# A fused layer on one core: two tiles' statistics first, pair 0's keys in other PSUM banks, and another order of the transfers ahead of the expert loop

## The reference

```
g = x[:, :, curve[:, 1], curve[:, 0]]                 # 256 pixels of each image
h = concat([einsum('bcn,ec->bne', g, proj_w) + proj_b, txt], 1)   # 4 x 768 x 192
n = layernorm(h)
Q, K, V = xpos(n @ Wq), xpos(n @ Wk), n @ Wv          # 6 heads, 128 / 64
s = Q K^T / sqrt(128) * decay_mask                    # causal, no softmax
a = groupnorm(s V) * silu(n @ Wg) @ Wo
h = h + a
n = layernorm(h)
z = n P[s]                                            # 8 sub-layers of rank 16
w = softmax(top4(z C[s]^T))                           # 4 of 64 experts
y = sum_k w_k (gelu(z W1[k] + b1) W2[k] + b2)
out = h + gelu(concat_s y @ G1 + g1b) @ G2 + g2b
```

## Time and profile before

| | us |
|---|---|
| median of 3 runs | 892.36 |
| lowest, highest | 890.64, 892.42 |
| the profiled execution | 895.4 |
| its span | 893.6 |

### The profile page before, as it was taken

The page is one execution under the profiler, slowest core; times in us unless marked ns, Lnnn a source line. Parts: engine busy times, 40 slices in busy tenths (PEclk is TensorE's granted clock), DMA queues, the critical chain, the costliest instruction groups (busy, mean ns, idle before and its releaser), DMA issues.

```text
span 893.6 us, 16290 instructions
## 1 busy us (share of the span) xinstructions
PE 847.4 (95%) x5430; PEld 393.1 (44%) x5430; DVE 661.7 (74%) x1609; ACT 593.3 (66%) x901; POOL 528.8 (59%) x481
## 2 busy tenths in 40 slices
PE   8799999999999986998999999999999999999997
PEld 3477777777778755222223222322232223222222
DVE  5666666565476776888878887888788887877774
ACT  2243333335542472989897989798979897988784
POOL 0456565445365633575957595759575767575552
PEclk9999999999999998799999999999999999999998
DMA  9600002000000078889878887988788888889772
GB/s 257 235 1 1 2 2 76 2 1 1 1 2 16 15 113 197 252 251 264 247 225 258 270 252 234 262 269 246 248 249 273 251 270 249 267 268 285 246 253 98
DMA packets 90116, 154.28 MB, mean 173 GB/s; under 512 B 30329, under 2 KB 56377, under 8 KB 89644
## 3 DMA queue, kind: packets, MB, share of 16 engines
q1 hardware_dynamic: 90034, 153.25, 58.3%
HBM read 138.96 MB, written 15.83 MB: 173 GB/s over the span
## 4 chain that ended last, share of the span: by engine, by line
PE 75%; ACT 11%; DVE 7%; DMA 3%; issue 3%; SPq 1%; POOL 0%; DVEq 0%; POOLq 0%; ACTq 0%
PE ps L917 17%; PE ps L854 17%; PE ps L512 5%; PE ps L893 5%; PE ps L535 3%; PE ps L520 3%; PE ps L608 3%; PE ps L545 2%; PE ps L599 2%; ACT ring L1253 2%; DMA wbc<-w_rows 2%; PE ps L577 2%; PE ps L687 1%; PE ps L656 1%; PE ps L708 1%
## 5 line engine op out<-in xcount | busy, mean ns | idle before, releaser
L1958 POOL TENSOR_TENSOR ring<-ring,wbc 128x512 f32<-128x512 f32 x192 | 245.5, 1280 | 151.6 <-ACT ring L1262 139.7
L1740 DVE TENSOR_TENSOR ring<-ps,ring 128x1024 f32<-128x1024 f32 x192 | 234.7, 1222 | 81.0 <-PE ps L893 52.2
L854 PE MATMUL ps<-zst,w1st 99*128 99x512 bf16 x768 | 213.5, 389 | 21.4 <-ACT ring L1253 10.7
L1253 ACT ACTIVATE ring<-ps 128x1024 f32<-128x1024 f32 x192 | 196.7, 1025 | 16.7 <-PE ps L854 16.6
L917 PE MATMUL ps<-ring,w2cur 128*32 128x512 f32 x1536 | 205.2, 607 | 0.0
L1264 ACT ACTIVATE ps<-ps 128x512 f32<-128x512 f32 x192 | 112.9, 588 | 55.0 <-PE ps L854 54.9
L1743 DVE TENSOR_TENSOR ring<-ps,wbc 128x512 f32<-128x512 f32 x192 | 130.9, 682 | 1.7 <-DMA wbc<-w_rows 1.6
L854 PEld LDWEIGHTS ps<-zst,w1st 99*128 99x128 bf16 x768 | 61.5, 98 | 143.3 <-issue 44.5
L1262 ACT ACTIVATE ring<-ps 128x512 f32<-128x512 f32 x192 | 116.4, 606 | 0.1
L1806 POOL TENSOR_TENSOR s2q<-s2q,rope 128x768 f32<-128x768 f32 x24 | 43.1, 1820 | 90.4 <-ACT s2q L1061 90.4
L893 PEld LDWEIGHTS ps<-wst,sel 32*128 32x128 bf16 x384 | 18.1, 91 | 148.9 <-DVE ring L1740 94.0
(11 more groups left out here) (192 smaller groups left out, 1290.1 us busy)
## 6 DMA issues: line engine op xcount, KB each, us to landing
wbc<-w_rows SPq DMA_DIRECT2D x192, 512.0 KB, 5.6
w2cur<-in_w SPq DMA_DIRECT2D x48, 256.0 KB, 4.8
w_parts<-wp SPq DMA_DIRECT2D x72, 64.0 KB, 3.3
zst<-z_parts SPq DMA_DIRECT2D x72, 64.0 KB, 5.0
w1st<-w_parts SPq DMA_DIRECT2D x12, 256.0 KB
wst<-w_parts SPq DMA_DIRECT2D x24, 128.0 KB, 4.2
z_parts<-zp SPq DMA_DIRECT2D x6, 384.0 KB, 5.5
wst<-w_parts SPq DMA_DIRECT2D x24, 96.0 KB, 4.0
```

The costliest lines, as they stand in the source:

```text
L854: return pe.matmul(bank(to), w1st[0:99, 4 * a + j, col:col + P], zst[0:99, (i // 2) % 2, j, :], start=True, stop=True)
L1253: act.activation(ring[:, slot:slot + 2, :].rearrange("p a n -> p (a n)"), ps[:, 0:2 * BLK], ACT.Gelu_apprx_tanh).then_inc(s["duo_gelu"], 1)
L1740: dve.tensor_tensor(v, ps[:, WBANK * 512:WBANK * 512 + 1024], v, ALU.mult).then_inc(s["duo_done"], 1)
L1958: pool.tensor_tensor(ring[:, slot, :], ring[:, slot, :], wbc[:, g % 4, 1, :], ALU.mult).then_inc(s["tri_done"], 1)
```

## The change

In the front DVE takes the statistics of tiles 0 and 1 alone and normalises pair 0; the other 22 tiles' statistics follow, and both `rotate_queries` of pair 0 stand ahead of `xn_make(1)`. ACT does `swap(0, 0)` and `swap(0, 1)` ahead of the second square root and of the table load for Silu. Pair 0's keys go to banks 4 to 7 and wait for no `rq` or `sq`; its values wait for those, its gates for nothing, and stand ahead of `xn_turn(1)`, which waits for `rk` 2. `keep_warm(2, 4)` becomes one matmul of 256 columns.

Ahead of the loop: tile 3's parts get their own place in `zp2`, and `z_high(2)`, which writes there next, waits for their store; SP's order changes; `load_ones(1)` has its own semaphore, awaited in group 16; on DVE `largest(3)` and `mark(3)` stand ahead of `variances(4, 12)`, the masks and `outputs` ahead of `chosen_exps(3)` and `normaliser(3)`; on PE `turn_gates(3)` stands behind `turn_x2(2)` and `(3)`, `gn_spread` directly behind `gn_mean`, `wo_pair(6)` ahead of `project_z(2)`; `keep_gates(3)` behind the `x2_out` pair on ACT. In the loop one `keep_clock` matmul is added at i = 2, n = 4.

```diff
+        def key_bank(k):
+            return 0 if k else 4
...
         def wp_of(tile):
+            if tile == 3:
+                return zp2[:, :, 0:2 * P].rearrange("p k (a n) -> p k a n", a=2)
...
-                             t["ones"][:, 1024 * m:1024 * m + 1024]).then_inc(s["ld_late"], 16)
+                             t["ones"][:, 1024 * m:1024 * m + 1024]).then_inc(s["ld_ones" if m else "ld_late"], 16)
...
             store_rows(2)
-            store_rows(3)
-            store_gates(2)
-            store_gates(3)
             sp.wait_ge(s["aq"], TILES)
             sp.wait_ge(s["ak"], TILES)
             attention_over(sp)
             sp.wait_ge(s["wo_s"], PAIRS // 2)
             sp.dma_start(sel[:, :, :]...
+            store_rows(3)
+            store_gates(2)
+            store_gates(3)
...
-            for g in range(3):
+            for g in range(4):
                 spread(g)
...
             load_gates(0)
+            load_w1(sp, 1)
             load_ones(1)
-            load_w1(sp, 1)
...
-                if g + 3 < GROUPS:
+                if 0 < g < GROUPS - 3:
                     spread(g + 3)
...
-            keep_warm(2, 4)
+            keep_warm(1, 4, 256)
...
                 for x in range(2):
-                    if x == 0:
+                    if k > 0 and x == 0:
                         pe.wait_ge(s["rq"], 2 * k + 2)
-                    else:
+                    if k > 0 and x == 1:
                         pe.wait_ge(s["sq"], 2 * k + 2)
-                    whole(2 * x, k, x, QK, QK)
-                rest(0, 2, k, QK, QK).then_inc(s["k_full"], 1)
+                    whole(key_bank(k) + 2 * x, k, x, QK, QK)
+                rest(key_bank(k), 2, k, QK, QK).then_inc(s["k_full"], 1)
...
-                pe.wait_ge(s["rk"], 2 * k + 1)
+                    pe.wait_ge(s["rq"], 2)
+                    pe.wait_ge(s["sq"], 2)
+                else:
+                    pe.wait_ge(s["rk"], 2 * k + 1)
...
                 values(k)
+                if k == 0:
+                    gates(0)
+                    pe.wait_ge(s["rk"], 2)
...
-            pe.wait_ge(s["wT_done"], 3)
-            turn_gates(3, 1)
             pe.wait_ge(s["g_out"], TILES)
             turn_x2(2, 2)
             turn_x2(3, 3)
+            pe.wait_ge(s["wT_done"], 3)
+            turn_gates(3, 1)
             keep_clock(1)
             gn_mean(1, 6)
+            gn_spread(1, 6)
             project_z(1, 7)
             turn_x2(4, 2)
-            gn_spread(1, 6)
             turn_x2(5, 3)
...
             scores(4, 0)
+            wo_pair(6, 4)
             project_z(2, 7)
-            wo_pair(6, 4)
...
-            pe.wait_ge(s["ld_late"], 16 * 3)
+            pe.wait_ge(s["ld_late"], 16 * 2)
...
                 if g == 16:
                     pe.wait_ge(s["ld_scr1"], 16 * 9)
+                    pe.wait_ge(s["ld_ones"], 16)
...
+                    if i == 2:
+                        keep_clock(1, PBANK)
                     scores(tile + 1, PBANK)
...
             def z_high(blk):
                 act.wait_ge(s["z_e"], blk + 1)
+                if blk == 2:
+                    act.wait_ge(s["w_stored"], 48 * 4)
...
-            ln_root(1, 0, 4)
+            ln_root(1, 0, 2)
             xn_out(0)
-            ln_root(2, 4, TILES)
+            swap(0, 0)
+            swap(0, 1)
+            ln_root(2, 2, TILES)
...
-            variances(0, 4)
-            inverses(1, 0, 4)
+            variances(0, 2)
+            inverses(1, 0, 2)
...
+            xn_make(0)
+            dve.wait_ge(s["ld_text"], 64)
+            tile_stats(texts)
+            dve.wait_ge(s["image"], 4)
+            tile_stats((2, 3, 12, 13, 14, 15))
+            dve.wait_ge(s["ld_rope0"], 16)
+            rotate_queries(0, 1)
+            dve.wait_ge(s["st1"], TILES)
+            variances(2, TILES)
+            rotate_queries(0, 0)
+            inverses(2, 2, TILES)
...
+            dve.wait_ge(s["st2"], 6)
+            variances(4, 12)
+            mask(PAIRS - 1, 0)
+            mask(PAIRS - 1, 1)
+            shifts(4, 4, 12)
             chosen_exps(3)
+            outputs(PAIRS - 1, 0)
             normaliser(3)
...
-                if tile > 0:
+                if tile > 0 and tile != 3:
                     pool.wait_ge(s["w_stored"], 48 * before(tile))
```

More of the change, by code:

```diff
@@ L184, in fused_layer @@
         block = ctx.enter_context(nc.Block())
-        names = ("zeroed ld_img ld_text ld_row ld_col ld_wblk ld_q ld_k ld_vg ld_rope0 ld_rope1 ld_small ld_osc fill_set ld_mid ld_late ld_final ld_bias ld_sel ld_w1 ld_scr0 ld_scr1 st_w1 st_z hot seen picked_s pix_t pixt_s img image "
+        names = ("zeroed ld_img ld_text ld_row ld_col ld_wblk ld_q ld_k ld_vg ld_rope0 ld_rope1 ld_small ld_osc fill_set ld_mid ld_late ld_ones ld_final ld_bias ld_sel ld_w1 ld_scr0 ld_scr1 st_w1 st_z hot seen picked_s pix_t pixt_s img image "
                  "st1 st2 ln_var ln_std ln_done xn_d xn_t xn_e "
@@ L462, in _, with keep_warm @@
         def _(pe):
-            def keep_warm(n, to):
+            def keep_warm(n, to, cols=512):
                 for _ in range(n):
-                    pe.matmul(bank(to), vn[:, 0, 0:2, :].rearrange("p e v -> p (e v)"),
-                              vn[:, :, :, :].rearrange("p a e v -> p (a e v)")[:, 0:512], start=True, stop=True)
+                    pe.matmul(bank(to, 0, cols), vn[:, 0, 0:2, :].rearrange("p e v -> p (e v)"),
+                              vn[:, :, :, :].rearrange("p a e v -> p (a e v)")[:, 0:cols], start=True, stop=True)
             pe.wait_ge(s["fill_set"], 1)
@@ L571, in gates @@
             def gates(k):
-                pe.wait_ge(s["rk"], 2 * k + 2)
+                if k > 0:
+                    pe.wait_ge(s["rk"], 2 * k + 2)
                 for x in range(2):
@@ L791, in _ @@
                     xn_turn(k + 1)
-                gates(k)
+                if k > 0:
+                    gates(k)
                 if k == 9:
@@ L802, in _, with keep_clock @@
             scores(3, 0)
-            def keep_clock(n):
+            def keep_clock(n, to=7):
                 for _ in range(n):
-                    pe.matmul(bank(7), ident[:, :], cblk[:, :], start=True, stop=True)
+                    pe.matmul(bank(to), ident[:, :], cblk[:, :], start=True, stop=True)
             turn(PAIRS - 1, 1)
@@ L1162, in _ @@
                     keep(p, 1)
-                swap(k, 0)
-                swap(k, 1)
+                if k > 0:
+                    swap(k, 0)
+                    swap(k, 1)
                 if k == 1:
@@ L1211, in _ @@
             x2_make(3, 2)
-            keep_gates(3, 1)
             x2_out(2, 2)
             x2_out(3, 3)
+            keep_gates(3, 1)
             x2_make(4, 2)
@@ L1323, in _ @@
             texts = [tile for tile in range(TILES) if tile % 12 >= 4]
-            dve.wait_ge(s["ld_text"], 64)
-            tile_stats(texts[0:6])
-            dve.wait_ge(s["image"], 2)
-            tile_stats(range(4))
+            dve.wait_ge(s["image"], 1)
+            tile_stats(range(2))
             def variances(a, b):
@@ L1366, in xn_make @@
                 ins.then_inc(s["xn_d"], 1)
-            xn_make(0)
-            dve.wait_ge(s["image"], 4)
-            tile_stats(texts[6:])
-            tile_stats(range(12, 16))
-            dve.wait_ge(s["st1"], TILES)
-            variances(4, TILES)
-            inverses(2, 4, TILES)
-            dve.wait_ge(s["ld_rope0"], 16)
             def rotate_queries(k, x):
@@ L1392, in rotate_keys @@
                 c = k % CH
-                src = ps[:, 2 * x * 512:2 * x * 512 + QK].rearrange("p (h d) -> p h d", d=DQK)
+                at = (key_bank(k) + 2 * x) * 512
+                src = ps[:, at:at + QK].rearrange("p (h d) -> p h d", d=DQK)
                 dve.wait_ge(s["k_full"], k + 1)
@@ L1619, in _ @@
                     residual(4, 7)
-                rotate_queries(k, 1)
-                rotate_queries(k, 0)
+                if k > 0:
+                    rotate_queries(k, 1)
+                    rotate_queries(k, 0)
                 if last:
```

8 lines of the change are left out of this document (1 added, 7 removed).

## The result

The changed kernel takes 882.63 us in the median (881.56 to 885.56, 4 runs), the kernel before beside it 892.39. The ratio is 0.990, with a 95% interval of 0.987 to 0.993. The profiled execution is 883.18 (span 881.4), against 895.4: -12.2 from one to the other, where the prediction's sum said -15.1. The time is inside the range, 5 us above the predicted one. Ratios compare fast runs alone; one slow run of the kernel before (1607.26 us, beside experiment 12) is left out. Of the three terms the front gave -3.8 (said -6.7), the stretch ahead of the loop -6.1 (said -7.6), the loop -2.3 (said -0.8).

The account below looks back on a forecast made before the run. PE was taken as the bound, with 75% of the span. Front -6.7, ahead of the loop -7.6 and loop -0.8 made -15.1 against 895.4: 880.3, or 877.3 for the median (chance 0.62); range 870.5 to 885.0.

Parts of the forecast that it names:

- Shift through attention: Between front and loop, from 50 to 310 us: a shift won in the front should arrive whole ahead of the loop.
- (a): Front: ACT's first square root moves from 19.53 to 18.25, -1.3 us, and pair 0's queries end at 25.6.
- (c): Front: DVE becomes the bound; `xn_make(1)` runs 31.0 to 32.1, rotation ends at 35.8, pair 1's transpose comes 5.4 us earlier.
- Rival A: Front: queries and keys run at 1.2 GHz, so the front gives -3.5 and the time is 880.5; chance 0.15.
- (b): Front: pair 0's keys in banks 4 to 7 wait for nothing and run from 25.6 to 29.8: -7.1 us.
- (d): Front: gates no longer stand between pair 1's transpose and queries; transpose to first query takes 1.3 instead of 3.5: -2.2 us.
- (e): Ahead of the loop: earlier `gn_spread` -2.1, earlier masks -0.9; PE's last projection ends at 346.5 rather than 349.1.
- (f): Ahead of the loop: POOL's 6.8 us wait goes; the third `wst` piece is issued at 340.9 and lands at 349.0.
- rival B: Ahead of the loop: a transfer still ends last, loop start gains only -4.2 and the time is 880.7; chance 0.18.
- (h): Ahead of the loop: `z_high(2)`'s new wait costs nothing, as tile 3's store lands by about 334 and ACT arrives at 336.
- The loop: In the loop: the added `keep_clock` matmul gives between -1.7 and +1.0 us, taken as -0.8; ACT bounds the first 12 us.
- C: In the loop: the clock stays low, costing 2.3 us more per group; with 8 such groups 895; chance 0.03.

Follow-up runs that it names:

- experiment 12: Changed kernel with experiment 8's front, Experiment 4's order, experiment 5's place and `w1st` parts stacked in DRAM for fewer, wider transfers; median 877.46 us, ratio 0.981 to the kernel before.
- Experiment 1: Changed kernel with the two full-width fillers, `keep_warm(2, 4)`, put back in the front; 880.87 us in one execution.
- experiment 2: Changed kernel with DVE's `variances(2, TILES)` moved ahead of `rotate_queries(0, 1)`; 880.31 us in one execution.
- Experiment 4: Changed kernel with SP issuing `ones`, `zst` and `wst` right after `spread(0)`, ahead of what groups 1 to 3 need; 884.64 us in one execution.
- 7: Changed kernel with tile 3's gate parts back in the buffer shared with tile 2 and without `z_high(2)`'s wait; 888.63 us in one execution.
- experiment 5: Changed kernel with Experiment 4's order and the second half of `w1st` issued earlier, where attention's last tile is rotated; 884.42 us in one execution.
- experiment 8: Changed kernel with the edits of Experiment 1 and experiment 2, plus ACT's second root ahead of pair 0's swaps and `xn_make(1)` ahead of its query products; 880.30 us, one execution.

## Why the prediction was right, and where its sizes were off

**Shift through attention.** Right: -3.81 at pair 0's heads, -3.81 at the last pair's.

**(a), the first root.** 18.11, said 18.25. Right. But "I charge 0.9, half of what the keys lost before" was the first mis-sized term: queries end at 28.1, said 25.6, so 2.5 were lost to the clock. That is 1.6 of the 2.9 by which the front's -6.7 became -3.8; DVE's order (c) is the rest. Experiment 1 gives back only 0.8, since its cure costs 1.5 itself. Rival A named this mechanism; that its -3.5 is near the measured -3.8 is luck, since it had queries and keys wholly at the lower clock (4.1 lost) and nothing lost on DVE beyond the forecast. The prediction also weighed a rule of the Trainium skill, "TensorE: Matmul & The Clock Gate", Part 4, that transposes don't count as PE being busy. Here the clock stayed at 0.50 through the transpose and through another 4.4 us of unbroken ordinary matmuls (21.6 to 26), which neither bears the rule out nor contradicts it; no run here separates them.

**(b), the keys.** Right in kind: no wait, 2.85 and 1.56 us at full clock. **(d)** too: transpose to first query 1.34, said 1.3.

**(c), DVE.** The step that failed as written is "So I let it begin at 31.0": the block by POOL was foreseen, on `xn_make`, and it fell on two operations of `variances` ahead of the second `rotate_queries`. On `xn_make` it would have delayed `rotate_keys` alone; here it also held the values on PE. The keys' rotation started at 35.8, said 32.1; experiment 2 puts 1.5 of it on the order, the rest is the late queries. The Trainium skill ("SBUF — State Buffer", Who interferes with whom) gives the condition: a DVE instruction with two SBUF inputs meets a GpSimd instruction that reads SBUF, and the loser waits for the whole of it. L1357 has two SBUF inputs and fits, at 1.71 for 0.2. L1358 was held as long (1.70) with one, and `xn_make` has one too, so this condition doesn't cover them.

**(e), spread and masks.** Right in the sum: `gn_var` 3.0 earlier beyond the front's shift, projections 2.9 (said 3.0 and 2.6). Its two parts cancel by luck: `gn_aggr` came 1.4 earlier (said 0.9), and from there to `gn_var` 1.6 were won (said 2.1).

**(f), the transfers.** The third `wst` piece was issued at 337.96; with the front's 3.8 added back that is 341.8, said 340.9. It landed in 8.9, said 7.9. The prediction's sum has two slips here: 336.3 and the 4.8 from the first `zst` to the third `wst` give 341.1, not 340.9, and 356.8 - 349.0 is 7.8, not 7.6. So the issue was 0.7 late and the landing 1.0, and from -7.8 these 1.7 lead to the measured -6.1. Against the stated -7.6 that is 1.5, somewhat less than half of the way to rival B. Experiment 4 shows that transfers end last there, and 7 that without tile 3's own place the start is 7.3 later. The chosen value stood for a landing as before, but `w1st`'s half had moved in front of `ones` and close behind `wst`, on full engines (share 1.12 from 342 to 346 us); that this is what delayed the piece isn't shown.

**(h), at nothing.** Right: tile 3's last store landed at 329.7, and ACT made the copy behind 332. Its condition was the right one to name: experiment 5 took the cover off, and the wait of 8.8 us then ended last ahead of the loop, through DVE's residual, a path the prediction didn't name.

**The loop.** The added matmul was taken at half of 1.7; it gives 1.5. The other 1.0, from the shorter stretch at half clock in the first groups, was no term, for "but ACT bounds them" was wrong: 2.1 us less of that stretch gave 1.0, and in experiment 8, which starts 2.7 earlier but has the clock back only 0.5 earlier, 2.2 us more of it cost 1.0.

**Forecast, rivals and luck.** C did not happen, A and B half did. The measured median is nearer to 883.9, the time of A and B together, than to the forecast's 877.3. Of the 5.3 between forecast and median 2.9 are the sum's (883.18 against 880.3), and 2.4 come from "The median of the runs is 3.0 below that execution": here it is 0.55 below. The median is inside a range of 14.5 us partly by luck: the front and the stretch ahead of the loop lacked 4.4, and the loop won back 1.5 of it by more than its term.

Two signs of being wrong were missed narrowly: PE's idle time ahead of the loop is 2.52 and 1.38 together (sign: over 4 us), and heads start at 45.8 (sign: later than 46). The third came: a stretch of half clock in the loop, at 763.3 to 766.7, that the trace of before doesn't have. The range has slips of its own: its lower end moves the sum's by 2, its upper end (885.7 to 885.0) by 0.7, and the front's fast end would be -9.1 (-7.6 and the block's 1.5) where it took -8.8.

## What to carry to other kernels

When a start waits for a transfer, add up what the engines have to move in that stretch before changing its order: other orders moved the wait from ahead of the loop to groups 4 to 12, to the stores, or to groups 8 to 16, and only a cheaper transfer removed it. Look at GB/s beside the share of busy transfer engines; full engines at a third of the rate of their neighbours were here transfers of 16 partitions in short pieces. When a chain is shortened, look at where each engine's small operations now fall against POOL's long ones, and put them into time in which the engine waits anyway.
